# A two-layer transformer on one core: first feed-forward's down products moved into the second layer's input stage, delta rule and attention due times set anew

## The reference

```python
h = silu(x @ gate.T) * (x @ up.T)           # 16 pieces of 128 x 512 in the kernel
h = h * rsqrt(mean(h * h) + eps)            # a factor for each token
y = y + h @ w_down.T                        # first feed-forward, down products
xn = layernorm(y); q, k, v = rmsnorm(xn) @ (w_q, w_k, w_v)   # layer 1, input stage
h1 = gelu(xn @ w1.T + b1)                   # second feed-forward, up products
```

## Time and profile before

| | us |
|---|---|
| median of 3 runs | 1585.38 (1580.24 to 1586.68) |
| the profiled execution, its own time | 1581.93 |
| its span, first to last instruction | 1580.2 |
| PE busy | 1423.2 (90%) |
| VectorE, ScalarE, GpSimd busy | 1047.3, 854.7, 531.8 |
| mean granted clock of TensorE | 0.947 of full speed |

### The profile page before, as it was taken

How to read it: one execution, slowest core, us unless ns; L and a number is a source line. 1 busy time by engine, 2 the same in 40 slices (tenths; PEclk the granted TensorE clock), 3 DMA queues, 4 the chain that set the end, 5 groups by cost and what they waited for, 6 DMA issues and landing times. The chain is left out here.

```text
span 1580.2 us, 35680 instructions
## 1 busy us (share of the span) xinstructions
PE 1423.2 (90%) x13996; PEld 1056.1 (67%) x13996; DVE 1047.3 (66%) x2150; ACT 854.7 (54%) x1728; POOL 531.8 (34%) x562
## 2 busy tenths in 40 slices
PE   4469999999999999999999999999899967888998
PEld 3345767777776877777687777777678844554855
DVE  6977685876868587685858768586745373663344
ACT  4345655655666565666656565665455135665210
POOL 3841333242333324232332323234245266340100
PEclk9678999999999999999999999999999987999899
DMA  5112111120112112010211201111320120001100
GB/s 170 45 35 47 33 25 41 27 45 10 31 24 37 43 25 45 9 35 20 37 43 25 46 9 37 30 25 29 91 68 1 54 75 0 2 1 34 48 8 20
DMA packets 142485, 56.39 MB, mean 36 GB/s; under 512 B 109776, under 2 KB 134992, under 8 KB 142064
## 3 DMA queue, kind: packets, MB, share of 16 engines
q1 hardware_dynamic: 133424, 48.20, 13.3%
q10 hardware_dynamic: 8896, 5.91, 1.2%
HBM read 37.11 MB, written 16.97 MB: 34 GB/s over the span
## 5 line engine op out<-in xcount | busy, mean ns | idle before, releaser
L1147 POOL TENSOR_TENSOR og<-og,sz 128x256 f32<-128x256 f32 x128 | 93.1, 728 | 565.4 <-DVE og L1090 343.9
L684 PE MATMUL banks<-wz,xT 128*128 128x256 f32 x512 | 137.9, 416 | 13.8 <-DVE yacc L1110 13.8
L937 DVE SCALAR_TENSOR_TENSOR Yv<-banks,cwall,Yv 128x511 f32<-128x511 f32 (+2 forms) x192 | 129.3, 739 | 12.1 <-ACT Yv L777 12.1
L540 PE MATMUL banks<-wv,xT 128*128 128x512 f32 x256 | 122.0, 621 | 5.0 <-DVE Yv L937 5.0
L684 PEld LDWEIGHTS banks<-wz,xT 128*128 128x128 f32 x512 | 99.6, 204 | 39.1 <-issue 24.9
L540 PE MATMUL banks<-wqk,xT 128*128 128x512 f32 x256 | 125.4, 617 | 0.3 <-DVE Yk L937 0.2
L755 PE MATMUL banks<-wo,oT 128*128 128x256 f32 x512 | 122.9, 383 | 0.3 <-ACT oT L929 0.3
L924 ACT ACTIVATE junk<-og 128x512 f32<-128x512 f32 x64 | 40.4, 631 | 120.0 <-POOL og L1147 119.9
L755 PEld LDWEIGHTS banks<-wo,oT 128*128 128x128 f32 x512 | 94.2, 193 | 12.1 <-ACT oT L929 0.8
L1154 POOL TENSOR_TENSOR rn<-ss,c_half 128x4 f32<-128x4 f32 x64 | 64.5, 1007 | 100.1 <-DVE ss L1104 100.0
L1864 DVE TENSOR_REDUCE mx<-banks 128x1 f32<-128x128 f32 (+3 forms) x128 | 58.3, 488 | 54.1 <-PE banks L1787 51.6
(11 more groups left out here) (369 smaller groups left out, 3644.9 us busy)
## 6 DMA issues: line engine op xcount, KB each, us to landing
cm_d<-CM SPq DMA_DIRECT2D x32, 256.0 KB, 4.3
wqk<-in_L_attn_W_qkvz SPq DMA_DIRECT2D x8, 512.0 KB, 4.5
wv<-in_L_attn_W_qkvz SPq DMA_DIRECT2D x8, 512.0 KB, 4.6
wz<-in_L_attn_W_qkvz SPq DMA_DIRECT2D x16, 256.0 KB, 2.9
wo<-in_L_attn_W_out SPq DMA_DIRECT2D x16, 256.0 KB, 3.1
blk<-cm_d SPq DMA_DIRECT2D x128, 16.0 KB, 1.8
t_d<-tb SPq DMA_DIRECT2D x16, 128.0 KB, 1.7
Td<-t_d SPq DMA_DIRECT2D x128, 16.0 KB, 1.8
```

Source lines behind the costliest of these rows:

```text
L540: ins = pe.matmul(bank[b][:, :], xT[:, d, b * S + of_batch, :], w[:, d, :], start=(d == 0), stop=(d == KD - 1))
L684: ins = pe.matmul(bank[7][:, b * 256:(b + 1) * 256], xT[:, d, b * S + q, :], wz[:, d, :], start=(d == 0), stop=(d == KD - 1))
L937: v.scalar_tensor_tensor(y, bank[b][:, 0:T - j], conv_w(k, t)[:, 3 - j:4 - j], y, ALU.mult, ALU.add).then_inc(s["tap"].sem, 1)
L1147: pool.tensor_tensor(og[:, n, :, :], og[:, n, :, :], sz[q % 2][:, b, :].rearrange("p (h d) -> p h d", h=VR), ALU.mult).then_inc(s["osz"].s ...
```

## The change

1. **Down products.** L1357 to L1367, L1416, L1433 and L1439 leave the delta rule part. The input stage begins with them in another form. ScalarE copies each of the 16 hidden pieces, rounded to float32r (`act_high`); the rests are taken by VectorE (12, `v_low`) and GpSimd (4, `pool_low`); PE multiplies both by the weights in float32r, 128 products of 128x256 (`pe_down0`). Buffers are placed anew so that the pieces live across the barrier.
2. **Input stage by pairs.** Statistics, power, normalisation, turns, rotation and the splits run for one pair of tiles at a time, behind that pair's down products, in the order of a new table `LIN` (its numbers are ranks 0.4 apart over all engines). The DMA issues of ScalarE's queue go to SyncE's.
3. **Due times of the delta rule.** `TURN`, `FSTEP`, `AT`, `FIRST`, `FINAL`, `START` all have new numbers; no instruction of the turns is added or removed.
4. **Attention.** The due times of scores, maxima, exponentials and value products are given for each width; the table is new. No instruction is added or removed.

The diff, cut to its core (`AT` by its first and fourth lines; new functions that only carry over old instructions by pairs left out):

```diff
-TURN = 69.77
-FSTEP = 7.25
+TURN = 69.22
+FSTEP = 7.14
...
+    "g": 79.32, "wqk": 140.6, "wv": -14.88, "cm": 201.39, "base": 147.71, "wz": 210.16, "E0": -32, "E1": -34.07, "E2": -42.83, "E3": -138.23, "exp0": -32.46, "exp1": -404.76, "exp2": -110,
...
+    "pq3": -278.11, "q0": 19.61, "q1": 20.5, "q2": -199.91, "q3": -274.53, "qs": 29.08, "qT0": 25.89, "qT1": -236.89, "sq0": -39.95, "sq1": -111.72, "nq": 33.04, "QK0": 31.43, "QK1": -12.12,
...
-        pe.wait_ge(*s["f0w2"]())
-        for i in range(4):
-            yield START["f0"] + FSTEP * (17 + i)
-            if i == 2:
-                pe.wait_ge(*s["f0ms"]())
-            for u in range(2):
-                b, t = divmod(2 * i + u, QT)
-                for f in range(8):
-                    ins = pe.matmul(bank[i][:, u * D:(u + 1) * D], hidden(8 * b + f)[:, t * P:(t + 1) * P], down_f[f // 4][:, f % 4, :], start=(f == 0), stop=(f == 7))
-            ins.then_inc(s["f0dn"].sem, 1)
...
+        for t, name, landed in ((an, "attn_norm_w", s["l1an"]), (mn, "moe_norm_w", s["l1s"])):
+            for k in range(KD):
+                sp.dma_start(t[:, k:k + 1], a["L1_attn_" + name][k * P:(k + 1) * P].rearrange("(p o) -> p o", o=1)).then_inc(landed.sem, 16)
+            if t is an:
+                sp.dma_start(cos[:, :, :], a["rope_cos"].rearrange("(q p) e -> p q e", p=P)).then_inc(s["l1s"].sem, 16)
+                sp.dma_start(sin[:, :, :], a["rope_sin"].rearrange("(q p) e -> p q e", p=P)).then_inc(s["l1s"].sem, 16)
+        sp.dma_start(b2[:, :], a["L1_ffn_b2"].partition_broadcast(P)).then_inc(s["l1s"].sem, 16)
...
+    def act_high(act):
+        for n in range(16):
+            yield LIN[f"hi{n}"]
+            act.copy(h_hi[:, n, :], hidden[:, n, :]).then_inc(s["fhi"].sem, 1)
+
+    def v_low(v):
+        for j, n in enumerate(by_vector):
+            yield LIN[f"lo{n}"]
+            v.wait_ge(*s["fhi"](n))
+            v.tensor_tensor(h_lo[:, n, :], hidden[:, n, :], h_hi[:, n, :].bitcast(F32), ALU.subtract).then_inc(s["flo"].sem, 1)
+
+    def pool_low(pool):
+        for j, n in enumerate(by_pool):
+            yield LIN[f"lp{n}"]
+            pool.wait_ge(*s["fhi"](n))
+            pool.tensor_tensor(h_lo[:, n, :], hidden[:, n, :], h_hi[:, n, :].bitcast(F32), ALU.subtract).then_inc(s["flp"].sem, 1)
...
+    def pe_down0(pe, i):
+        b = i // 2
+        yield LIN[f"dn{i}"]
+        if i >= 2:
+            pe.wait_ge(*s["fy"](2 * (i - 2) + 1))
+        for u in range(2):
+            t = (2 * i + u) % QT
+            for part in (h_hi, h_lo):
+                for f in range(8):
+                    n = 8 * b + f
+                    if i % 2 == 0 and u == 0:
+                        pe.wait_ge(*(s["fhi"](n) if part is h_hi else lo_made(n)))
+                    elif u == f == 0 and part is h_hi:
+                        pe.wait_ge(*lo_made(8 * b + 6))
+                        pe.wait_ge(*lo_made(8 * b + 7))
+                    ins = pe.matmul(bank[6 + i % 2][:, u * D:(u + 1) * D], part[:, n, t * P:(t + 1) * P], down[:, f, :], start=(part is h_hi and f == 0), stop=(part is h_lo and f == 7))
+        ins.then_inc(s["fdn"].sem, 1)
+
+    def v_pair(v, i):
+        yield LIN[f"y{i}"]
+        if i == 0:
+            v.wait_ge(*s["fr"]())
+        v.wait_ge(*s["fdn"](i))
+        for u in range(2):
+            t = 2 * i + u
+            v.scalar_tensor_tensor(xa[:, t, :], bank[6 + i % 2][:, u * D:(u + 1) * D], rt[:, t:t + 1], xa[:, t, :], ALU.mult, ALU.add).then_inc(s["fy"].sem, 1)
+        yield after(i, "st")
+        v.wait_ge(*s["fy"](2 * i + 1))
+        for t in range(2 * i, 2 * i + 2):
             ins = v.bn_stats(bn[:, t, :], xa[:, t, :])
...
+    def pool_x_parts(pool, i):
+        yield after(i, "xhi")
+        pool.wait_ge(*s["xTe"](2 * i + 1))
+        pool.tensor_copy(x_part[0][:, :, two(i), :], xT[:, :, two(i), :]).then_inc(s["xhi"].sem, 1)
+        yield after(i, "xlo")
+        pool.wait_ge(*s["xhi"](i))
+        pool.tensor_tensor(x_part[1][:, :, two(i), :], xT[:, :, two(i), :], x_part[0][:, :, two(i), :].bitcast(F32), ALU.subtract).then_inc(s["xlo"].sem, 1)
...
     def pe_qkv(pe, i):
-        if i == 0:
-            pe.wait_ge(*s["wq"]())
+        yield after(i, "qkv")
+        pe.wait_ge(*s["wq"]())
         pe.wait_ge(*s["xTe"](2 * i + 1))
...
+    def streams(engine, by_pair, others):
+        in_order([(0.0, f(engine, i)) for i in range(QT) for f in by_pair] + [(0.0, f(engine)) for f in others])
+
+    def on_tensor(pe):
+        streams(pe, (pe_down0, pe_turned_x, pe_qkv), (pe_squares, pe_hidden, pe_turned_keys))
...
-ROUND = 13.0
-UNIT, WAVE = 0.68, 1.46
+ROUND = 13.39
+UNIT, WAVE = 0.36, 0.58
 ATTN = {
-    "slot": -2.29, "split": 4, "T1": 2.39, "T1c": 2.97, "max": 6, "N": 17.56, "T2": 19.95, "T2c": 20.77, "exp": 21.92, "expc": 22.61, "pv": 25.2, "oTc": 34.48, "oTt": 34.75, "on": 35.53,
+    "slot": -2.29, "split": 4, "T1": -0.74, "T1c": 3.41, "max0": 7.32, "max1": 8.15, "max2": 9.49, "max3": 12, "mx0": 24.94, "mx1": 33.37, "mx2": 34.23, "mx3": -54.06, "N": -10.98,
+    "T2": 21.14, "T2c": 25.31, "exp0": 22.69, "exp1": 25.07, "exp2": 26.37, "exp3": 30.2, "expc0": 29.1, "expc1": -40.95, "expc2": 30.52, "expc3": 32.83, "pv0": 25.85, "pv1": 30.32,
+    "pv2": 15.75, "pv3": 35.32, "oTc": 41.98, "oTt": 37.09, "on": 62.01,
 }
...
-            yield ATTN["max"] + UNIT * i
+            yield ATTN[f"max{t}"] + UNIT * g
...
-            yield ATTN["exp"] + WAVE * i
+            yield ATTN[f"exp{kt}"] + WAVE * gp
...
-            yield ATTN["max"] + UNIT * (i + 1)
+            yield ATTN[f"mx{t}"] + UNIT * g
```

More of the change, by code:

```diff
@@ new lines, in pool_low, with pe_squares @@
+    def pool_low(pool):
[3 more added lines that the diff above has]
+            pool.tensor_tensor(h_lo[:, n, :], hidden[:, n, :], h_hi[:, n, :].bitcast(F32), ALU.subtract).then_inc(s["flp"].sem, 1)
+    def pe_squares(pe):
+        yield LIN["ss"]
+        for t in range(TT):
+            ins = pe.matmul(bank[0][:, t:t + 1], squares[:, t // QT, t % QT * P:(t % QT + 1) * P], c["ones"][:, 0:1], start=True, stop=True)
+        ins.then_inc(s["fss"].sem, 1)
@@ L1616, in act_turned_x @@
[L1616 to L1636 removed]
+        v.wait_ge(*s["ag"](i))
@@ new lines, in pe_turned_x, with act_turned_x @@
+    def pe_turned_x(pe, i):
+        yield after(i, "xT")
+        if i == 0:
+            pe.wait_ge(*s["fms"]())
+        for t in range(2 * i, 2 * i + 2):
+            pe.wait_ge(*s["x"](t))
+            pe_turned(pe, s, "xTt", c, bank, xn, t, "xTe")
+    def act_turned_x(act, i):
+        for u in range(2):
+            yield LIN[f"xTe{2 * i + u}"]
+            act.wait_ge(*s["xTt"](2 * i + u))
+            act.copy(xT[:, :, 2 * i + u, :], bank[u][:, 0:D].rearrange("p (k t) -> p k t", k=KD)).then_inc(s["xTe"].sem, 1)
@@ L1647, in pe_qkv, with v_rope @@
             ins.then_inc(s["qkv"].sem, 1)
-    def on_tensor(pe):
-        for t in range(TT):
-            pe.wait_ge(*s["x"](t))
-            pe_turned(pe, s, "xTt", c, bank, xn, t, "xTe")
-            if t % 2 and t >= 3:
-                pe_qkv(pe, t // 2 - 1)
-        pe_qkv(pe, QT - 1)
-        for n in range(14):
-            pe_hidden(pe, n)
-        pe.wait_ge(*s["ks"]())
+    def v_rope(v, i):
+        yield after(i, "rope")
+        v.wait_ge(*s["qkv"](2 * i + 1))
+        v.wait_ge(*s["rot"](i))
+        if i:
+            v.wait_ge(*s["rope"](i - 1))
+        v.tensor_tensor(ro[0][:, :, :, :], half(i, 0), turns(csr, i), ALU.mult)
+        v.tensor_tensor(ro[1][:, :, :, :], half(i, 1), turns(snr, i), ALU.mult)
+        v.tensor_tensor(ro[2][:, :, :, :], half(i, 0), turns(snr, i), ALU.mult)
+        v.tensor_tensor(ro[3][:, :, :, :], half(i, 1), turns(csr, i), ALU.mult).then_inc(s["ro"].sem, 1)
+        v.wait_ge(*s["ro"](i))
+        v.tensor_tensor(qk[:, two(i), :, 0:HD:2], ro[0][:, :, :, :], ro[1][:, :, :, :], ALU.subtract)
+        v.tensor_tensor(qk[:, two(i), :, 1:HD:2], ro[2][:, :, :, :], ro[3][:, :, :, :], ALU.add).then_inc(s["rope"].sem, 1)
+        for n in range(2):
+            yield after(i, f"sub{n}_")
+            v.wait_ge(*s[f"part{n}"](i))
+            v.tensor_tensor(flat[:, two(i), :], flat[:, two(i), :], parts[:, n, two(i), :], ALU.subtract).then_inc(s[f"sub{n}"].sem, 1)
@@ new lines, in v_zero, with act_values @@
+    def v_zero(v):
+        yield LIN["qz"]
+        v.memset(qs[:, :, :, :], 0.0).then_inc(s["qz"].sem, 1)
+    def act_values(act, i):
+        yield after(i, "vp")
+        if i == 0:
+            act.wait_ge(*s["slots"](0))
+        act.wait_ge(*s["ro"](i))
+        for u in range(2):
+            act.activation(vp[:, 2 * i + u, :, 0:HD], qkv(i)[:, u, QK * HD:QK * HD + KVH * HD].rearrange("p (g e) -> p g e", g=KVH),
+                           ACT.Copy, scale=r8[:, 2 * i + u:2 * i + u + 1]).then_inc(s["vp"].sem, 1)
@@ new lines, in act_parts, with pool_keys @@
+    def act_parts(act, i):
+        for n in range(3):
+            yield after(i, f"part{n}_")
```

(10 more changed lines are left out.)

300 lines of the change are left out of this document (133 added, 167 removed), and 83 rows, old and new, of tables (AT, FINAL, FIRST, LIN).

## The result

| | before | after |
|---|---|---|
| median of 14 runs each, us | 1584.28 | 1575.45 |
| after to before, 95% interval | | 0.9948 (0.9924 to 0.9972) |
| the profiled execution, its own time | 1581.93 | 1568.21 |
| its span | 1580.2 | 1566.5 |

The account below looks back on a forecast made before the run. Barriers make each part its own term; PE bounds the delta rule, while input stage, seam and attention have something to give. 1581.9 - 15 - 6 - 6.5 = 1554.4, forecast as 1555 us; 8 in 10 for 1541 to 1571.

Parts of the forecast that it names:

- The seam: Delta rule's end to attention's start: without down products the input stage starts 25 us earlier but carries more; -15 us.
- The tail of ternary weights: End of the delta rule part: last comparisons, turn, copy and write of ternary weights end at 1243, input stage starts at 1244.
- The stage: Input stage, now with the down products: 60 us long, with dn0 ending at 9.6 and qkv0 starting at 25.
- the first rival: Input stage: VectorE and GpSimd get in each other's way, price 4 and 3 us more, total 1562; chance 0.17.
- Attention: Attention's new order: rounds of 13.4 us, 0.95 less in each of 7 rounds; -6.5 us, bounds -9 and +3.
- paced by VectorE's maxima: Attention: m0 to m11 come in one run that waits for VectorE's maxima, set against the gain from covered waits.
- The covers that the prediction names: Attention, each round: T2b's wait of 1.13 us for the copy, T1b and the output's turn, 0.4 each, are covered.
- The delta rule: Its new due times: -0.3 us a turn over 14 turns, -2 for first and last; -6 us in all.
- most waits keep their neighbours: Delta rule's turns: sorted by due time, most waits stay as they were; one of 0.25 us a turn is covered.
- The first turn and the last ones: Delta rule's first and last turn, where PE idles for 38 and 9 us: -2 us together.
- The new orders give nothing: Delta rule and attention, both retimed, stay as now and only the -15 us remain: 1567; chance 0.13.
- The bound of +8 for the delta rule: Upper bound of the delta rule's -6 us: as much the other way at fewer places; lower bound -14.

Follow-up runs that it names:

- e1: The changed kernel with all of the delta rule's due times as in the kernel before: 1557.5 us, ratio 0.9836 to before.
- g2: The changed kernel with the loads of key, value and feed-forward weights waiting for the running turn's first inversion block: 1565.2 us, ratio 0.9884 to before.
- h6: The changed kernel, new times kept, with the first inversion block in two halves and other work between, in all turns but the first: 1563.9 us.
- h4: The changed kernel with the delta rule's old times and the first inversion block in two halves, except in first and last turns: 1548.3 us, ratio 0.976.
- e6: The changed kernel with the first feed-forward's hidden products due 6.5 us earlier, the parts of its input made as early as before: 1583.8 us.
- e7: The changed kernel with the last turn's value products and output product due just ahead of the first inversion block: 1581.5 us.

## Why the prediction was wrong, step by step

**The seam: right, 2.5 us short.** The tail of ternary weights was to take from 1230.6 to 1243, 12.4 us, and 1 us more for the barrier; it took 13.7 (1247.67 to 1261.4, ScalarE's first copy). The stage was to take 60, it took 62.5, dn0's end and the start of qkv0 9.7 and 28.0 us into it where 9.6 and 25 were said. In between the first pair was normalised 18.1 into it where 14 was said, by the first rival's mechanism:

```profile
1275.51 3.51 POOL L1770 MEMSET ks<- 128x4096 bf16 x1
...
1275.60 3.89 DVE L1619 TENSOR_SCALAR l_xn<-yacc,mv,rs 128x256 f32<-128x256 f32 x2 [0.81 <-POOL rs L1627]
...
1279.31 0.73 PE L1470 MATMUL banks<-c_ident,l_xn 128*128 128x128 f32 x4 [4.39 <-DVE l_xn L1619]
...
1282.62 2.05 DVE L1619 TENSOR_SCALAR l_xn<-yacc,mv,rs 128x256 f32<-128x256 f32 x2 [0.81 <-POOL rs L1627]
```

```profile
L1619 DVE TENSOR_SCALAR l_xn<-yacc,mv,rs x8: 397/598/3570, 1275.6 to 1296.3; 128x256 f32<-128x256 f32 x8
```

One normalisation takes 0.40 undisturbed. The first pair takes 3.89 beside GpSimd's memset, one of its two alone 3.57; the second pair takes 2.05 beside GpSimd's split of `xT`; and TensorE, whose dn2 stands behind the turn of the first pair, is idle for 4.39. The Trainium skill (SBUF — State Buffer, SBUF: two separate sides) has the pair of ports that the two share as an exclusive lock, held for a whole instruction by the one that starts first. By that rule the held operation can't end before the memset does, and the trace agrees: the memset ends at 1279.02, the held operation at 1279.17. The trace of before had it already: one of the eight normalisations (L1548) took 3.67 beside a memset of 3.65, and the prediction counted the memset in GpSimd's queue alone. The rival's price of 7 was too high: VectorE lost 3.1 and 1.3 us in these two pairs, and the whole stage is 2.5 over what was said.

**Attention: right in what, mis-sized.** The step that was mis-sized is "paced by VectorE's maxima, and for those PE waits 14.1 already". The row under it in the earlier trace rows is PEld's: the queue that loads weights waits there, ahead of a busy TensorE. PE's own wait for maxima was 1.0 in the same stretch before and is 2.3 after (attention's stretch, before and after):

```profile
PE banks L1786 <- DVE mx L1864: 1.0, 5, 0.2
PE banks L1880 <- DVE mx L1958: 2.3, 12, 0.2
```

The covers that the prediction names come to 1.13 + 0.4 + 0.4 = 1.93 a round, of which it kept 0.95 because of the maxima; the rounds fell by 2.0 (14.35 to 12.34). With seven rounds at 2.0 the term would have been -14, and -18 with what lies at both ends.

**The delta rule: wrong, in sign, and the step that failed.** Measured +17.1 by the marks and +18 by e1, where -6 was said. "No work goes", "most waits keep their neighbours" and -0.3 a turn was a balance of waits, taken from the orders of TensorE, VectorE and ScalarE. Three things were missing in it:
- SyncE's order in the turns. The prediction says nothing of it, but the new tables put the weights' loads behind `Td`'s pieces, just ahead of the block, and the feed-forward's 2.5 MB as well. The stops at the block were in the trace of before (10.4 us, "issue"), and it didn't read them: it has the idle rest "spread over small waits". Its own two turns of the earlier trace rows differ by 1.66 us, 67.99 against 66.33, and that is one stop:

```profile
650.11 0.39 PE L595 MATMUL banks<-Td,CM 32*32 32x32 f32 x24 [1.67 <-issue]
```

  Moving the loads behind the block gave 10 of the 18 us by the medians (g2).
- The clock behind a stop: 1.7 us behind the one that was read, nothing behind some others (below).
- The first turn and the last ones, costed together at -2. They cost 3.4 to 5.0 (marks of after, h6 against h4) and 3.8 to 9.5 (h6 against h4, after against e1). In the last turn the cause is only half known: neither the late filler nor the block's place explains it (e6, e7), and what is left there with the loads moved, 4.6 us (g2 against e1), stays open.

That steady turns without a stop stay as they were within 0.5 us nearly held: 66.8 to 67.8 at a clock of 1.00 against 66.3 to 67.9, and 0.6 a turn in h6 against h4, with 2 us more of stops in h6's. "The new orders give nothing", at 0.13, was the nearest rival, but none had them lose on one side and gain on the other. The bound of +8 for the delta rule was "as much the other way at fewer places", a guess by symmetry; what g2 gives back by moving the loads, 10, is more than that.

**The sum** had three terms of the same sign, and the range was made as if they could only fail a little, each for itself. The errors partly cancelled, by luck: the delta rule was 23 us worse than said and the seam 2.5, attention 12 better. With the measured terms in its place: 1581.9 - 12.5 - 18.3 + 17.1 = 1568.2, the profiled time; the median lies 7 above that profile, where before's lay 2 above its own.

## What to carry to other kernels

Read the order of the queue that only issues transfers as carefully as those that compute: a load that lands early enough can still stand at the wrong moment. A wait named "issue" inside a run of small instructions is a place to put other work: here it gave 9 to 11 us, as much as the whole change.
